# A decoder's expert stage: fp32 products replaced by three products of rounded halves, with the weights split ahead of time

## Chip, cores and metric

One NeuronCore of a Trainium2 chip runs the whole program as one launch. The metric is the device time of that launch in microseconds (us). TensorE is called PE (its weight loads PEld), VectorE DVE, ScalarE ACT, GpSimd POOL, and SyncE SP, which here issues most transfers.

## What is computed

The reference is a two-layer decoder on x of 4 x 512 tokens by 512 features: self-attention, cross-attention and a mixture of experts, then a second self-attention, cross-attention and a ternary feed-forward net. The change touches the mixture of experts and the first self-attention, in which its weights are prepared. The expert part, cut:

```python
h = x @ down_w + down_b                    # 512 -> 256
probs = softmax(x @ router_w + router_b - COST_LAMBDA * cost)
topv, topi = top_k(probs, 2); gate = softmax(topv)
for k in range(2):                         # 8 experts, hidden sizes 256, 512, 768, 1024, twice
    acc = sum over e of gelu(gelu(h * mask_e) @ w1_e + b1_e) @ w2_e + b2_e
    out = out + acc * gate[..., k]
```

All of it is fp32.

## The kernel before

The program is a row of stages. The profile has them at about these times: self-attention 0 from 0 to 460 us, cross-attention 0 to 540, mixture of experts to 1135, self-attention 1 to 1975, cross-attention 1 to 2640, the ternary net to the end.

The mixture routes 4096 token rows (2048 tokens, two experts each). It sorts them by expert into tiles of 256 rows (at most 23 and one spare, 24 turns in all) and cuts each expert's hidden layer into pairs of 128 columns. An *item* is one tile against one pair: `ITEMS` is 79, always. `which` holds, for each item, its tile and its pair, found on the chip.

- **Weights.** `pack_experts` (L781), called by GpSimd in self-attention 0, copies each of the 20 pairs from the inputs to `moe_items` in DRAM, 60 transfers. `load_item` (L974) on SP loads one item's first weight (L979) and its second weight with the bias (L982) into one of `SLOTS` = 3 buffers. The first half waits for `hidden` of item i-3, the second for `output` of item i-3.
- **Rows.** `turn_rows` on PE (L1154) transposes a tile; DVE's `keep_turned` (L1476) copies it from PSUM to `turned`. ACT's `take_tile` (L1253) copies the item's tile to `x_now`.
- **Products.** In PE's queue, item i's turn of the loop is `hidden(i + 1)` (L1165), then `output(i)` (L1176). Between the two of one item ACT applies Gelu (L1264). Each has four fp32 products of 256 columns, which the profile shows as two instructions each.
- **Sums.** DVE adds each item's result to its tile's row of `acc` (L1510), which GpSimd cleared before the loop (L1580). SP stores one tile of `acc` to `moe_mixed` (L993) when all its items are in, 23 times. After the loop GpSimd gathers each token's two rows (L1601).
- **Beside it.** In the same loop GpSimd loads one eighth of a ternary weight (L1591, 512 KB, 24 in all), DVE turns it into ternary form every third item (L1491 to L1497), and GpSimd stores it (L1589, 256 KB).

SP's queue in the loop is written out by hand; every wait in it holds up what stands behind it:

```python
            for i in range(SLOTS, ITEMS):
                if i + AHEAD < TILES:
                    load_rows(i + AHEAD)
                load_item(i)
                if (stored + 1) * max(PAIRS) + SLOTS <= i:
                    store_tile(stored)
                    stored += 1
```

In self-attention 0 GpSimd has, in this order, the split of `wo` into halves (L472, L474), which ACT waits for before its 7th copy of turned probabilities (L363), the small power of the first layer norm (L96), which DVE waits for, and then `pack_experts`.

Of the kernel before, what the change touches and what calls it, by code (L numbers as in the profile page):

```python
# [133 lines left out]
def self_attention_0(nc, m, x, Wq, bq, Wk, bk, Wv, bv, Wo, bo, packed, a):  # L134
# [18 lines left out]
    NEXT_X = TILES + 6  # L153
    Q0, SC = NT, TILES + 2 * NT
    TA, TV, MM = TILES // 2, TILES // 2, 3 * KD + 2 * GROUPS + NT
    with ExitStack() as ctx:
# [34 lines left out]
        s.out_rows_in, s.out_high, s.out_low, s.out_stored = (sem(n) for n in ("out_rows_in", "out_high", "out_low", "out_stored"))  # L191
        w_q, w_k, w_v, w_out, x_tok_loaded = sem("w_q"), sem("w_k"), sem("w_v"), sem("w_out"), sem("x_tok_loaded")
# [4 lines left out]
        def _(sp):  # L197
# [8 lines left out]
            sp.dma_start(m.x_tok[:], x.rearrange("b (j p) d -> p (b j) d", p=P)).then_inc(x_tok_loaded, 16)  # L206
# [16 lines left out]
            with sp.Fori(0, B - 1) as b:  # L223
                sp.wait_ge(x_tok_loaded, 16)
                sp.wait_ge(s.mm.full, b * MM + 3 * KD + 1)
                sp.dma_start(x_rows[:], m.x_tok[:, bass.ds(b * NT + NT, NT), :]).then_inc(s.x_loaded, 16)
                load_out(b)
                store_out(b)
# [153 lines left out]
        def _(dve):  # L382
            with dve.Fori(0, B) as b:
# [57 lines left out]
                dve.wait_ge(x_tok_loaded, 16)  # L441
# [27 lines left out]
        def _(pool):  # L469
            pool.wait_ge(w_out, 32)  # L470
            pool.wait_ge(s.max_ready, 1)
            pool.tensor_copy(wo_high[:], wo[:]).then_inc(s.wo_high_made, 1)  # L472
            pool.wait_ge(s.wo_high_made, 1)
            pool.tensor_tensor(wo_low[:], wo[:], wo_high[:].bitcast(F32), ALU.subtract).then_inc(s.wo_split, 1)  # L474
            layernorm_rstd(pool, st, 0, m, s)
            pack_experts(pool, packed, a)
# [283 lines left out]
FIRST = KL * LATENT  # L760
# [3 lines left out]
class Packed:  # L764


    def __init__(self, nc, ctx):
# [6 lines left out]
        self.wo1 = nc.dram_tensor("split_out", (HEADS1, P, 2, D), F32, kind="Internal").ap()  # L774
        self.items_in, self.cleared = ctx.enter_context(nc.semaphore("moe_items_in")), ctx.enter_context(nc.semaphore("moe_cleared"))


ITEM_LOADS = 3 * sum(PAIRS) * 16


def pack_experts(pool, packed, a):  # L781

    for e in range(EXPERTS):
        for n in range(PAIRS[e]):
            to, at = packed.items[PAIR0[e] + n], slice(n * 2 * P, (n + 1) * 2 * P)
# [47 lines left out]
def mixture_of_experts(nc, m, w, packed, a):  # L833
# [27 lines left out]
    with ExitStack() as ctx:  # L861
# [101 lines left out]
        def _(sp):  # L963
# [38 lines left out]
            for i in range(1, SLOTS):  # L1002
                load_item(i)
# [1964 lines left out]
```

## Time and profile before

| | us |
|---|---|
| median of 3 runs | 2902.24 (2897.63 to 2905.83) |
| span of the profiled execution | 2871.8 |
| outside that span, by the median | 30.4 |
| item loop, first product to last | 773.5 to 1062.9 |

The profiled execution has no time of its own beside its span. The span runs from the first to the last instruction, so a change is added to the median as it is found in the span. An engine's busy time joins overlapping instructions of a group; products on PE overlap one another by most of their shown duration, so the step between them is read from runs of several.

### The profile page before, as it was taken

Reading aid. Unit: us, or ns where it says so; the run is one execution under the profiler, and the core shown is the slowest. Engines: PE = TensorE matmul, PEld = TensorE weight load, DVE = VectorE, ACT = ScalarE, POOL = GpSimd, SP = SyncE. Lnnn points to the kernel's source line nnn. Section 1 sums busy time; section 2 is a strip of 40 time slices with the busy share of each in tenths; the row PEclk is TensorE's granted clock in tenths of the full one; section 3 lists DMA queues with packets and bytes.
Section 4 is the critical chain, followed back from the end, with each engine's and each line's share of the span. In section 5 each row is a group of like instructions: output and inputs, shape, how many; then the busy total and the mean of one; then the engine's idle time right before and its main releaser. Section 6 shows DMA issues by size and latency. Waiting matters only on the chain. (4 is left out here: it accounts for less than half of the span.)

```text
span 2871.8 us, 40570 instructions
## 1 busy us (share of the span) xinstructions
PE 2673.5 (93%) x12750; PEld 1685.2 (59%) x12750; DVE 1806.2 (63%) x3475; ACT 1420.3 (49%) x2978; POOL 294.5 (10%) x399
## 2 busy tenths in 40 slices
PE   8999997979999987999999999997999999997898
PEld 4555554444588863677777777775545455443444
DVE  5666674654543326756755756754777777775676
ACT  4454463322133322554553653743577676664665
POOL 1230003001711114000000000001110101000000
PEclk9999998989999999999999999998899999999999
DMA  3395105541687754323223223211000000001000
GB/s 140 86 123 143 58 15 184 186 141 54 200 277 234 248 184 148 115 103 109 73 106 110 68 104 124 66 67 59 5 6 6 5 2 5 2 2 71 26 23 30
DMA packets 114169, 266.30 MB, mean 93 GB/s; under 512 B 14464, under 2 KB 37008, under 8 KB 113200
## 3 DMA queue, kind: packets, MB, share of 16 engines
q1 hardware_dynamic: 97152, 211.16, 22.2%
q0 software_dynamic: 16816, 52.64, 7.8%
q8 instruction: 104, 1.70, 0.2%
q14 instruction: 97, 0.79, 0.1%
HBM read 208.97 MB, written 58.48 MB: 93 GB/s over the span
## 5 line engine op out<-in xcount | busy, mean ns | idle before, releaser
L2506 DVE TENSOR_REDUCE x_neg_max<-bank 128x1 f32<-128x512 f32 x512 | 327.1, 684 | 99.7 <-PE bank L2351 99.2
L2458 ACT ACTIVATE x_weights<-bank 128x512 f32<-128x512 f32 x512 | 279.1, 599 | 127.8 <-PE bank L2362 122.9
L1885 ACT ACTIVATE a_probs<-bank,a_neg_max 128x128 f32<-128x128 f32 (+3 forms) x256 | 136.1, 532 | 206.0 <-DVE a_neg_max L1979 202.0
L1785 PE MATMUL bank<-a_x_high,a_weights 128*128 128x512 f32 x640 | 218.3, 404 | 8.2 <-DMA a_weights<-split_qkv 2.3
L109 PEld LDWEIGHTS bank<-all_ident,a_probs 128*128 128x128 f32 x1200 | 151.5, 140 | 85.0 <-issue 47.0
L109 PE MATMUL bank<-all_ident,a_probs 128*128 128x128 f32 x1200 | 193.3, 273 | 3.0 <-ACT a_probs_t L1877 2.2
L1877 ACT COPY a_probs_t<-bank 128x128 f32<-128x128 f32 (+3 forms) x256 | 107.6, 420 | 144.2 <-PE bank L109 143.8
L1820 PE MATMUL bank<-a_k_cols,a_q_cols 128*128 128x128 f32 (+3 forms) x512 | 176.7, 434 | 0.4 <-DVE a_q_cols L1928 0.2
L1849 PE MATMUL bank<-a_wo,a_att_high 128*128 128x512 f32 x512 | 162.1, 398 | 3.9 <-DVE a_q_cols L1928 2.9
L1510 DVE TENSOR_TENSOR moe_acc<-bank,moe_acc 128x512 f32 x79 | 54.6, 692 | 171.1 <-PE bank L1176 170.5
L1165 PE MATMUL bank<-moe_gh_cols,moe_item 128*128 128x256 f32 x632 | 151.8, 383 | 3.0 <-DMA moe_item<-moe_items 2.7
L1176 PE MATMUL bank<-moe_item,moe_wide 128*128 128x256 f32 x632 | 149.4, 379 | 0.0
L1832 PE MATMUL bank<-a_probs_t,a_v_rows 128*128 128x512 f32 (+3 forms) x512 | 148.6, 433 | 0.0
L1264 ACT ACTIVATE moe_wide<-bank,moe_item 128x256 f32<-128x256 f32 x158 | 66.3, 471 | 161.6 <-PE bank L1165 129.1
L1785 PEld LDWEIGHTS bank<-a_x_high,a_weights 128*128 128x128 f32 x640 | 121.3, 189 | 39.6 <-issue 6.2
L1891 ACT ACTIVATE a_probs<-a_probs,a_inv_sum 128x128 f32<-128x128 f32 (+3 forms) x256 | 142.0, 555 | 2.7 <-DVE a_inv_sum L1984 2.7
L2351 PE MATMUL bank<-x_k_cols,x_q_cols 64*128 64x512 f32 x512 | 136.6, 498 | 3.5 <-DVE x_neg_max L2506 3.4
L1979 DVE TENSOR_REDUCE a_neg_max<-bank 128x1 f32<-128x128 f32 (+3 forms) x256 | 125.7, 491 | 18.8
L2384 PE MATMUL bank<-x_weights,x_v_rows 128*17 128x512 f32 x1024 | 135.7, 603 | 0.0
L1165 PEld LDWEIGHTS bank<-moe_gh_cols,moe_item 128*128 128x128 f32 x632 | 118.1, 191 | 22.9 <-DMA moe_item<-moe_items 7.4
L2362 PE MATMUL bank<-x_q_cols,x_k_cols 64*128 64x512 f32 x512 | 128.1, 419 | 3.2 <-ACT x_weights L2458 2.8
L1176 PEld LDWEIGHTS bank<-moe_item,moe_wide 128*128 128x128 f32 x632 | 119.9, 190 | 16.8 <-issue 0.3
(413 smaller groups left out, 5437.0 us busy)
## 6 DMA issues: line engine op xcount, KB each, us to landing
a_weights<-split_qkv SPq DMA_DIRECT2D x80, 512.0 KB, 3.6
moe_item<-moe_items SPq DMA_DIRECT2D x79, 257.0 KB, 3.8
moe_item<-moe_items SPq DMA_DIRECT2D x79, 256.0 KB, 3.7
a_wo<-split_out SPq DMA_DIRECT2D x8, 2048.0 KB, 7.8
a_wo<-split_out SPq DMA_DIRECT2D x16, 1024.0 KB, 9.9
split_qkv<-x_qkv_parts SPq DMA_DIRECT2D x12, 1024.0 KB, 5.1
moe_items<-in_L_ffn_e_w POOLq DMA_DIRECT2D x40, 256.0 KB
split_out<-a_turned SPq DMA_DIRECT2D x8, 1024.0 KB, 4.0
```

The lines of the kernel that those rows point to most:

```text
L109: last = pe.transpose(bank[:, c * P:(c + 1) * P], rows[:, c * P:(c + 1) * P], ident)
L1165: last = pe.matmul(bank(("hidden", i))[:, c * TOKENS:(c + 1) * TOKENS], weight[:, k, c * P:(c + 1) * P], x_now[:, i % 2, k * TOKENS:(k + 1 ...
L1176: last = pe.matmul(bank(("item", i))[:, j * LATENT:(j + 1) * LATENT], hid[:, i % 2, c * TOKENS + j * P:c * TOKENS + (j + 1) * P], weight[: ...
L1785: last = pe.matmul(mm[g % 2], weight[:, k, :], x[:, k, :], start=n == 0, stop=n == 3 * KD - 1)
L1820: pe.matmul(sc[n % 4][:, 0:t], q_cols[:, h % 2, j * P:t], k_cols[:, h // GROUP, 0:t], start=True, stop=True).then_inc(s.sc.full, 1)
L1832: last = pe.matmul(mm[g % 2][:, c * P:], v_rows[:, c, kv * HD1:(kv + 1) * HD1], probs_t[:, n % 2, c, c * P:], start=c == 0, stop=c == NT - 1)
L1849: last = pe.matmul(mm[g % 2], att[:, at, j * P:(j + 1) * P], wo[:, at, part, :], start=h == first and att is att_high and part == 0, stop= ...
L1885: act.activation(probs[:, n % SLOTS, 0:t], sc[n % 4][:, 0:t], ACT.Exp, bias=neg_max[:, n:n + 1], accum_out=row_sum[:, n:n + 1]).then_inc(s ...
L1891: act.activation(probs[:, i % SLOTS, 0:t1], probs[:, i % SLOTS, 0:t1], ACT.Copy, scale=inv_sum[:, i:i + 1]).then_inc(s.probs_ready, 1)
L2351: pe.matmul(score_banks[slot % 3], q_cols[rows, u % 2, pair, j * P:(j + 1) * P], k_cols[rows, u % 2, pair, :], start=True, stop=True).then ...
L2458: act.activation(weights[:, chunk % 2, k, :], weight_banks[slot % 2], ACT.Exp).then_inc(s.weight.free, 1)
L2506: dve.tensor_reduce(neg_max[:, g % 2, j, h:h + 1], score_banks[slot % 3], AX.X, ALU.max, negate=True) \
```

## The change

Every expert weight w is kept as two halves, w_high (w rounded to the type `fp32r`) and w_low (w - w_high), and so are the item's input and its hidden values. A product becomes high x high + high x low + low x high, as products of type fp32r, which the kernel's other stages use already (L1785, L1849).

1. **Split, once.** `pack_experts` goes. In self-attention 0 GpSimd loads a pair (two transfers), casts 128x1024 to the high half, subtracts 128x1024 for the low half, stores 1 MB to `moe_items`, copies the bias by a fourth transfer, 20 times. The split of `wo` comes after the sixth pair, the first layer norm's power after the thirteenth. The staging buffers lie in `m.x_tok` of batches 1 to 3, so SP loads those parts of x only after the last pair is stored, ahead of `load_rows(1)`.
2. **Items.** `FIRST` doubles: an item's two loads are 512 and 513 KB. `hidden` and `output` have 12 products each in place of 4. PE now runs `hidden(i + 2)` ahead of `output(i)`; SLOTS stays 3.
3. **Halves of the activations.** ACT's `take_tile` writes x_high, GpSimd subtracts for x_low (128x512). DVE copies Gelu's result to hid_high and subtracts for hid_low (`split_hidden`).
4. **Sums.** DVE adds item i to a running sum in one of 4 slots (`add_result`); the running sum starts anew with each tile. SP stores every item's sum (256 KB, 79 stores). GpSimd's clearing of `acc` goes; small DVE work and one small PE product find the new places.
5. **Moves.** `keep_turned` from DVE to ACT, 5 tiles ahead. The bias of x (L1583, 4 x 128x2048 on GpSimd) to the routing phase. SP's first item loads wait for the last `core` product.

```diff
-FIRST = KL * LATENT
+FIRST = 2 * KL * LATENT
...
-        self.mixed = nc.dram_tensor("moe_mixed", (SPARE * TOKENS, LATENT), F32, kind="Internal").ap()
+        self.mixed = nc.dram_tensor("moe_mixed", (ITEMS * TOKENS, LATENT), F32, kind="Internal").ap()
...
+            def split_pair(i):
+                (e, n), stage = pairs[i], stages[i % STAGES]
+                pool.wait_ge(s.pair_in[i % STAGES], (i // STAGES + 1) * 32)
+                pool.tensor_copy(stage[:, :, 0].bitcast(F32R), stage[:, :, 1]).then_inc(s.pair_high, 1)
+                pool.wait_ge(s.pair_high, i + 1)
+                pool.tensor_tensor(stage[:, :, 1].bitcast(F32R), stage[:, :, 1], stage[:, :, 0], ALU.subtract).then_inc(s.pair_low, 1)
+                pool.wait_ge(s.pair_low, i + 1)
+                pool.dma_start(packed.items[i][:, 0:2 * FIRST], stage.rearrange("p w l n -> p (w l n)")).then_inc(s.pair_stored[i % STAGES], 16)
...
+            for i in range(len(pairs)):
+                if i == OUT_SPLIT_AT:
...
+                if i == FIRST_NORM_AT:
+                    layernorm_rstd(pool, st, 0, m, s)
+                split_pair(i)
+                if i + 2 < len(pairs):
+                    if i >= 1:
+                        pool.wait_ge(s.pair_stored[(i - 1) % STAGES], ((i - 1) // STAGES + 1) * 16)
+                    load_pair(i + 2)
...
             for i in range(SLOTS, ITEMS):
                 if i + AHEAD < TILES:
                     load_rows(i + AHEAD)
                 load_item(i)
-                if (stored + 1) * max(PAIRS) + SLOTS <= i:
-                    store_tile(stored)
-                    stored += 1
+                if i >= ACC_SLOTS:
+                    store_result(i - ACC_SLOTS)
...
                     for k in range(KL):
-                        last = pe.matmul(bank(("hidden", i))[:, c * TOKENS:(c + 1) * TOKENS], weight[:, k, c * P:(c + 1) * P],
-                                         x_now[:, i % 2, k * TOKENS:(k + 1) * TOKENS], start=k == 0, stop=k == KL - 1)
+                        for w, x in ((w_high, high), (w_high, low), (w_low, high)):
+                            last = pe.matmul(bank(("hidden", i))[:, c * TOKENS:(c + 1) * TOKENS], w[:, k, c * P:(c + 1) * P],
+                                             x[:, k, :], start=n == 0, stop=n == 3 * KL - 1)
+                            n += 1
...
             hidden(0)
+            hidden(1)
             for i in range(ITEMS):
...
-                if i + 1 < ITEMS:
-                    hidden(i + 1)
+                if i + 2 < ITEMS:
+                    hidden(i + 2)
                 output(i)
...
+            def split_hidden(i):
+                dve.wait_ge(*emptied(("hidden", i)))
+                if i >= 2:
+                    dve.wait_ge(*filled(("item", i - 2)))
+                dve.tensor_copy(hid_high[:, i % 2, :], hid[:, i % 2, :])
+                dve.drain()
+                dve.tensor_tensor(hid_low[:, i % 2, :], hid[:, i % 2, :], hid_high[:, i % 2, :].bitcast(F32), ALU.subtract).then_inc(s.hid_ready, 1)
+
+            def add_result(i):
+                to = acc[:, i % ACC_SLOTS, :]
+                if i >= ACC_SLOTS:
+                    dve.wait_ge(s.stored[i % ACC_SLOTS], i // ACC_SLOTS * 16)
+                dve.wait_ge(*filled(("item", i)))
+                dve.drain()
+                if i == 0:
+                    dve.tensor_copy(to, bank(("item", i))).then_inc(free(("item", i)), 1)
+                else:
+                    dve.scalar_tensor_tensor(to, acc[:, (i - 1) % ACC_SLOTS, :], same[:, i:i + 1], bank(("item", i)), ALU.mult, ALU.add) \
+                       .then_inc(free(("item", i)), 1)
...
+            for i in range(ITEMS):
+                pool.wait_ge(s.x_high_ready, i + 1)
+                tile = pool.value_load(which[i:i + 1, 0:1], min_val=0, max_val=SPARE)
+                pool.tensor_tensor(x_low[:, i % X_SLOTS, :], turned[:, bass.ds(tile, 1), :].rearrange("p o n -> p (o n)"),
+                                   x_high[:, i % X_SLOTS, :].bitcast(F32), ALU.subtract).then_inc(s.x_now_ready, 1)
+                q, late = divmod(i - QUANT_FROM - STORE_LAG, QUANT_EVERY)
+                if late == 0 and 0 <= q < EIGHTHS_ALL:
+                    store_ternary(q)
```

## Rows read from the trace of the kernel before

**Rows 1.** The page, section 1: engine busy time, share of span, instructions.

```profile
PE 2673.5 (93%) x12750; PEld 1685.2 (59%) x12750; DVE 1806.2 (63%) x3475; ACT 1420.3 (49%) x2978; POOL 294.5 (10%) x399
```

**Rows 2.** Timeline in the item loop: start, duration, engine, line, count.

```profile
954.49 1.89 PE L1165 MATMUL bank<-moe_gh_cols,moe_item 128*128 128x256 f32 x8
...
956.22 1.89 PE L1176 MATMUL bank<-moe_item,moe_wide 128*128 128x256 f32 x8
...
957.94 1.89 PE L1165 MATMUL bank<-moe_gh_cols,moe_item 128*128 128x256 f32 x8
958.28 0.33 SPq L982 DMA_DIRECT2D moe_item<-moe_items  x1
...
958.65 0.43 SPq L993 DMA_DIRECT2D moe_mixed<-moe_acc  x1
...
959.84 0.33 SPq L979 DMA_DIRECT2D moe_item<-moe_items  x1
```

**Rows 3.** Windows: us, busy time by engine, PE clock, transfer share, GB/s.

```profile
773.00:870.00 97.00, 96.78 (x482) 84.25 (x481) 44.32 (x70) 37.13 (x78) 21.21 (x19) 0.99 0.82 258
...
1136.00:1157.00 21.00, 17.23 (x74) 13.29 (x73) 12.18 (x18) 0.00 (x0) 0.00 (x0) 1.00 1.02 410
```

**Rows 4.** Transfers from 773 to 1062 us: 40 slices, sum, issues with landing.

```profile
DMA  5598988898777786877787877886887886776562
GB/s 158 168 340 257 315 294 260 298 272 281 254 226 236 237 272 210 273 228 214 237 257 215 275 245 215 258 240 206 267 262 233 243 272 175 268 253 215 172 201 73
DMA packets 37735, 69.19 MB, mean 239 GB/s; under 512 B 3824, under 2 KB 13643, under 8 KB 37707
...
moe_item<-moe_items SPq DMA_DIRECT2D x76, 257.0 KB, 3.8
...
ternary<-ew_down POOLq DMA_DIRECT2D x24, 256.0 KB, 2.7
...
ew_core<-in_L_ffn_w_gate POOLq DMA_DIRECT2D x8, 512.0 KB, 6.7
```

**Rows 5.** Transfers of the whole span: the projection weights of self-attention 1.

```profile
a_weights<-split_qkv SPq DMA_DIRECT2D x80, 512.0 KB, 3.6
```

**Rows 6.** Timeline: products of type fp32r, 512 columns wide.

```profile
1703.17 0.62 PE L1785 MATMUL bank<-a_x_high,a_weights 128*128 128x512 f32 x2
1703.63 0.39 PE L1785 MATMUL bank<-a_x_low,a_weights 128*128 128x512 f32 x1
```

**Rows 7.** Timeline: four transposes of type fp32r, 128 columns wide, seen by their loads.

```profile
1999.00 0.40 PEld L109 LDWEIGHTS bank<-x_ident_r,x_split 128*128 128x128 f32 x4 [1.15 <-DVE x_swapped L2544]
```

**Rows 8.** Groups on GpSimd: busy us, mean ns, idle before.

```profile
L2589 POOL TENSOR_TENSOR x_split<-x_rot,x_split 128x512 fp32r<-128x512 f32 x32 | 41.0, 1280 | 423.4 <-ACT x_split L2442 423.4
...
L787 POOL DMA_DIRECT2D moe_items<-in_L_ffn_e_w x20 | 14.1, 703 | 0.0
...
L474 POOL TENSOR_TENSOR a_wo_low<-a_turned,a_wo_high 128x2048 fp32r<-128x2048 f32 x1 | 4.6, 4614 | 0.1
...
L472 POOL CAST a_wo_high<-a_turned 128x2048 fp32r<-128x2048 f32 x1 | 1.9, 1890 | 55.2 <-DVE a_neg_max L411 55.2
```

**Rows 9.** Timeline of GpSimd in self-attention 0: the first layer norm's power.

```profile
126.04 1.03 POOL L96 TENSOR_TENSOR a_ln_rstd<-a_ln_var_eps,all_minus_half 128x4 f32<-128x4 f32 x1 [62.62 <-DVE a_ln_var_eps L86]
```

**Rows 10.** Timeline of ACT in self-attention 0: its seventh copy of turned probabilities.

```profile
71.99 0.59 ACT L366 COPY a_turned<-bank 128x512 f32<-128x512 f32 x1 [1.07 <-PE bank L109]
```

**Rows 11.** Timeline, GpSimd beside DVE at the loop's start.

```profile
765.81 18.01 POOL L1583 TENSOR_TENSOR all_x_tok<-all_x_tok,ew_up_b 128x2048 f32<-128x2048 f32 x4
...
781.81 2.04 DVE L1483 TENSOR_SCALAR all_scale<-moe_abs_total 128x3 f32<-128x3 f32 x1
...
783.92 0.18 DVE L1485 RECIPROCAL moe_inv_scale<-all_scale 128x3 f32<-128x3 f32 x1
```

**Rows 12.** Groups on DVE: busy us, mean ns, idle before.

```profile
L391 DVE TENSOR_TENSOR a_k_low<-a_whole,a_high 64x512 fp32r<-64x512 f32 x64 | 43.9, 686 | 12.4 <-ACT a_high L340 11.7
...
L1491 DVE TENSOR_SCALAR ew_core<-ew_core,moe_inv_scale 128x1024 f32<-128x1024 f32 x24 | 17.8, 744 | 0.0
```

More of the change, by code:

```diff
@@ L469, in _ @@
         def _(pool):
[L470 to L476, printed above, removed]
+            stages = [m.x_tok[:, NT * (1 + i):NT * (2 + i), :].rearrange("p j d -> p (j d)").rearrange("p (w l n) -> p w l n", w=2, l=2)
+                      for i in range(STAGES)]
@@ new lines, in _, with load_pair @@
+            pairs = [(e, n) for e in range(EXPERTS) for n in range(PAIRS[e])]
+            def load_pair(i):
+                (e, n), raw = pairs[i], stages[i % STAGES][:, :, 1]
+                at = slice(n * 2 * P, (n + 1) * 2 * P)
+                pool.dma_start(raw[:, 0].rearrange("p (k n) -> p k n", k=KL), chunked(a[f"L0_ffn_e{e}_w1"][:, at])).then_inc(s.pair_in[i % STAGES], 16)
+                pool.dma_start(raw[:, 1].rearrange("p (c n) -> p c n", c=2), chunked(a[f"L0_ffn_e{e}_w2"][at, :])).then_inc(s.pair_in[i % STAGES], 16)
@@ L774, in __init__ @@
         self.wo1 = nc.dram_tensor("split_out", (HEADS1, P, 2, D), F32, kind="Internal").ap()
+        self.pair_in = [ctx.enter_context(nc.semaphore(f"moe_pair_in_{i}")) for i in range(PAIR_STAGES)]
+        self.pair_stored = [ctx.enter_context(nc.semaphore(f"moe_pair_stored_{i}")) for i in range(PAIR_STAGES)]
         self.items_in, self.cleared = ctx.enter_context(nc.semaphore("moe_items_in")), ctx.enter_context(nc.semaphore("moe_cleared"))
[L778 to L785, printed above, removed]
-            half = KL * LATENT
-            pool.dma_start(to[:, 0:half].rearrange("p (k n) -> p k n", k=KL), chunked(a[f"L0_ffn_e{e}_w1"][:, at])) \
-                .then_inc(packed.items_in, 16)
-            pool.dma_start(to[:, half:2 * half].rearrange("p (c n) -> p c n", c=2), chunked(a[f"L0_ffn_e{e}_w2"][at, :])) \
-                .then_inc(packed.items_in, 16)
-            pool.dma_start(to[:, 2 * half:PACKED], columns(a[f"L0_ffn_e{e}_b1"][at]), allow_slow_non_contiguous=True) \
-                .then_inc(packed.items_in, 16)
+ITEM_LOADS, PAIR_STAGES = sum(PAIRS) * 16, 3
 def moe_weights(nc, ctx):
@@ L1124, in _ @@
             last.then_inc(full("gates"), 1)
+            pe.wait_ge(s.same_ready, 1)
+            pe.wait_ge(*room("same"))
+            pe.matmul(bank("same")[:, 0:P], ones[:], below[:], start=True, stop=True).then_inc(full("same"), 1)
             pe.wait_ge(s.gb1_ready, EXPERTS)
@@ L1158, in hidden @@
             def hidden(i):
-                weight = item[:, i % SLOTS, 0:KL * LATENT].rearrange("p (k n) -> p k n", k=KL)
+                weight = item[:, i % SLOTS, 0:FIRST].rearrange("p (l k n) -> p l k n", l=2, k=KL)
+                w_high, w_low = weight[:, 0], weight[:, 1]
+                high, low = (x.rearrange("p (k t) -> p k t", k=KL) for x in (x_high[:, i % X_SLOTS, :], x_low[:, i % X_SLOTS, :]))
                 pe.wait_ge(s.first_in[i % SLOTS], (i // SLOTS + 1) * 16)
@@ L1353, in _ @@
             dve.tensor_tensor(over, others, own, ALU.is_gt)
-            dve.tensor_tensor(same, others, own, ALU.is_equal)
+            dve.tensor_tensor(equal, others, own, ALU.is_equal)
             dve.drain()
-            dve.tensor_tensor(same, same, before[:].unsqueeze(1).to_broadcast(shape), ALU.mult)
+            dve.tensor_tensor(equal, equal, before[:].unsqueeze(1).to_broadcast(shape), ALU.mult)
             dve.drain()
-            dve.tensor_tensor(over, over, same, ALU.add)
+            dve.tensor_tensor(over, over, equal, ALU.add)
             dve.drain()
@@ L1462, in _ @@
                 add_magnitudes(SUMS_EARLY + t - EARLY, 1)
+            dve.wait_ge(*filled("same"))
+            dve.tensor_copy(same[:], bank("same")[:, 0:ITEMS]).then_inc(free("same"), 1)
             dve.wait_ge(*filled("const"))
```

231 lines of the change are left out of this document (149 added, 82 removed).

## The prediction, made before the changed kernel was run

> **What bounds the kernel now.** I read the page first: PE is busy for 93% of the span [rows 1], so any work taken from PE should show unless something else fills its place. Then I went to the stage that the change touches, by its timeline, since the mean over 2872 us says nothing about it. In the item loop the reader should look at the starts of PE's groups of eight: 954.49, 956.22, 957.94 [rows 2]. They are 1.73 us apart with no gap, 0.216 us for each instruction, so an item costs PE 16 x 0.216 = 3.46 us. 79 items make 273 us, and with the 20 tiles that are transposed inside the loop (8 x 0.11 us each) the 289 us from 773.5 to 1062.9 are explained. The loop is bound by PE and by nothing else.
>
> Next the transfers of the same stretch. They are not idle: 82% busy at 258 GB/s while PE is 100% busy [rows 3], and 69.19 MB move in the loop, 239 GB/s on average [rows 4]. An item's load takes 3.8 us from issue to landing [rows 4], longer than an item, and costs nothing only because SP issues it two items before PE needs it. This is the number I take the forecast from: a loop that is bound by PE, but with transfers near four fifths of what they can do.
>
> **The change on PE.** 24 products of type fp32r replace 16 fp32 instructions. The trace has none that is 256 columns wide. At 512 columns two of them start within 0.46 us, 0.23 each [rows 6]; at 128 columns four take 0.40 us with the whole first load counted, so 0.10 at most [rows 7]. A straight line between the two gives 0.14 us at 256 columns. From below, one of the two passes that an fp32 instruction of 256 columns makes takes 0.216 / 2 = 0.108 [rows 2]. I take 0.13: 24 x 0.13 = 3.1 us an item, between 2.6 and 3.4. By PE alone the loop would fall by 79 x 0.35 = 27 us (5 to 68).
>
> **The change in the transfers.** Per item, in KB of 1024 bytes: two loads of 512 and 513 in place of 256 and 257; one store of 256 in place of 23 in 79 items; the ternary work stays at (512 + 256) / 3 = 256. That is 1537 KB, 1.57 MB, where the loop moved about 0.88 MB an item. In all: 79 x 1025 + 79 x 256 + 24 x 768 + 24 x 256 = 125,775 KB. Three items, seven tiles of rows and two raw eighths (5891 KB) are in before the first product. 119,884 KB, 122.8 MB, are left. At PE's pace of 3.1 us an item this asks for 508 GB/s, at the old 3.46 still for 455.
>
> What can the transfers do? The same 4 KB runs, loads alone on SP's queue, reach 410 GB/s with the share at 1.02 [rows 3]. That is the most in this trace. In the item loop, where loads, stores and GpSimd's queue mix, the three slices with a 9 among the first nine moved 340, 315 and 272 GB/s [rows 4]. So a full queue of this mix is worth 0.30 to 0.37 MB/us, and I take 0.33, near the rows of the same mix and not near the pure one: 122.8 / 0.33 = 372 us for the loop (332 at 0.37, 409 at 0.30, 300 at 0.41).
>
> The Trainium skill (DMA: Bandwidth & Descriptors, Specifications) puts the HBM limit of one core at about 358 GB/s. By it the loop would be 122.8 / 0.358 = 343 us, an estimate. The 410 GB/s of the trace are above that limit, so it doesn't hold for one busy core here; my number doesn't use it.
>
> **The same from the order of SP's queue.** PE's order becomes hidden(i), output(i-2), hidden(i+1), output(i-1). SP issues, once output(i-3) has ended: the second half of item i, the store of item i-4, then the first half of item i+1. Let L be the time from output(i-3)'s end to the landing of that first half; hidden(i+1) needs it after only hidden(i) and output(i-2), one item's work, where before it was two. So two items take L plus one item's PE work: T = (L + 3.1) / 2. L: the second half's issue to the first half's issue is 1.56 us today with a store between [rows 2], some 0.15 for the semaphore, 3.6 for 512 KB on a quiet queue [rows 5], and what is in front of it: 512 + 256 KB at 410 GB/s are 1.9 us, of which 1.5 have passed, plus GpSimd's 256 KB an item, 0.6. Together 6.3, T = 4.7 us, 79 T = 371 us. Both ways meet at 372, 83 us more than 289 (43 to 120). The third buffer is used up here: it is SLOTS that would have to grow.
>
> **What hides in the loop.** With T = 4.7, DVE has per item a copy of 512 elements (0.37 by half of L1491's 1024, 0.69 at most), two operations of 0.69, and the ternary third, about 0.6: 2.4 us. GpSimd has 1.28 [rows 8] and 0.4 of issues; ACT two Gelus, a copy, 1.5. All fit. Their chain to the next product has more than one item of slack: at T = 3.1 the split after a ternary step would end 0.4 us before PE asks for it. Off the path, cost nothing; if DVE became late it would be by 0.3 to 0.7 us an item.
>
> **Self-attention 0.** A pair costs GpSimd a cast of 1024 (0.95, half of L472), a subtraction (2.3, half of L474) and four issues of 0.7: 6.1 us, 6.8 with waits [rows 8]. It waits for w_v, then for its own loads; I put the first pair's landing at about 23 us. Six pairs end at 64, the split of wo 6.5 later at 70.5. ACT needs it at 71.99 [rows 10]: no slack, and 0.5 us more a pair is 3 us of wait. Seven more pairs end at 118; the layer norm's power is wanted at 126.04 [rows 9], so 8 us of slack, but GpSimd's queue is strict: at 9 us a pair it comes at 152, and DVE, then PE's next projections, wait 26 us. The last seven pairs end near 175; x for batches 1 to 3 then loads before batch 1, of some 115 us, ends.
>
> There is a second cost. GpSimd's work and DVE's get in each other's way: while GpSimd adds over 128x2048, 18.01 us for four, DVE's scaling of 128x3 takes 2.04 us, where its neighbour in line takes 0.18 [rows 11]. The Trainium skill (SBUF — State Buffer, Who interferes with whom) says why: the two share one pair of ports, held by one for a whole instruction, against DVE instructions with two inputs in SBUF or in a two-port mode. The trace agrees. Which work is exposed: the subtractions L391, 0.69 each [rows 12], four to a projection of 3.43 us, so DVE is as full as PE there. With GpSimd holding 3.3 of 6.8 us, about 14 us of k projections in each of two batches stretch by a quarter: 7 us (0 to 14). With 3 us of waits for wo I take +10 (0 to 40). The 60 transfers that `pack_experts` made ran beside PE's work and nobody waited for them in this stage, so their going gives nothing.
>
> **Start of the loop.** ACT copies five tiles in place of DVE's four, and the first x_low adds 1.3 us on GpSimd: +3 (0 to 6). The first items (3 MB) load once the last core product has ended, 9 us of transfer at 0.33, while PE and DVE still work on the gates and the constant rows. The x bias and the clearing were hidden by PE in their old place and are in the new one. The end of the loop is the same chain: last sum, store, gather.
>
> **Sum.** 83 + 10 + 3 = 96 us in the span of 2871.8, so a span near 2968; the median is 30.4 above the span, 2902.2 + 96 = 2998.
>
> **Rivals.**
> - *A. Forecast: transfers and the lead of one item set the pace*, T 4.2 to 5.2. Chance 0.62. 2998.
> - *B. Transfers keep nearly their best rate*, 0.36 to 0.41 MB/us. For it: pure loads do 410 and two thirds of the bytes are of that kind. Against: the 3 us behind every issue stay, and a full mixed slice has not passed 340. Loop 300 to 341, with +13: 2926 to 2967, say 2948. Chance 0.17. The page's 358 GB/s ends here too.
> - *C. PE cools, or GpSimd is late in self-attention 0.* With 1.6 us of wait for every 4.7, PE may be granted its lower clock of 1.2 GHz, where its products double: 24 x 0.24 = 5.8 us, T up to 6. For it: the loop has held 0.99 only at 100% busy [rows 3], and no row shows it with such pauses. Against: it would still be busy for two thirds, with each pause under 2 us. A third of the loop so costs some 30 us more; the late power 26. 3030 to 3080, say 3055. Chance 0.14.
> - *D. The other side: the transfers are hidden and PE sets the pace.* T = 3.1 to 3.4, the loop 262 to 285: -27 + 13, about 2888. It needs 1.57 MB in less than 3.46 us, over 455 GB/s; below 440 (122.8 MB in 279 us) it can't be faster at all. The trace's best is 410 in pure loads. Chance 0.04 for faster and 0.03 for a draw.
>
> **Numbers.** The likeliest is 2998. B to 2940 and C to 3060 take in the bounds of the rate (0.41 leaves 2926 outside, 0.30 gives 3035) and of self-attention 0; about 2 in 10 stay out. Within 0.3% (9 us), which is about what this kernel's measurement can tell from no change: 0.03. Faster 0.04, slower 0.93.
>
> **What would show it.** In the profile after: the item loop 350 to 400 us long; transfer share at or near 1 there with 300 to 350 GB/s; PE idle before `hidden`, released by the transfer of moe_item, 1 to 2 us an item; product starts 0.12 to 0.14 us apart; the first half's landing 4.5 us or more; DVE's L391 in some places at 1 to 3 us; GpSimd's power at 126 to 130. Wrong would be: no wait for moe_item (then D), a rate over 380 GB/s (B), a PE clock under 0.9 in the loop or a wait of ACT or DVE for GpSimd over 10 us before 160 us (C).

## The result: 8% slower, outside the range

The changed kernel took 3133.27 us (median of 4 runs, 3132.12 to 3135.69) against 2900.43 for the kernel before: ratio 1.0795, 95% interval 1.0779 to 1.0812. Forecast were 2998 us and a range of 2940 to 3060. The direction and the place were right, the size was not: +233 us instead of +96.

The profiled execution of before was no typical one. Its span was 2871.8 us and its own time must have been near that, since in every later execution the time is the span plus some 1.8 us; the timed ones took 2898 to 2906. The prediction read this as 30 us "above the span". The likeliest reason is a difference between chips: on two chips the kernel before took 2860 to 2881 us, on two others 2891 to 2917. So stages are compared here with a second profile of both kernels from chips of the quick kind (`b1_before`, span 2868.5; `a2_after`, 3109.7). Starts in us:

| | before, first profile | b1_before | after, first profile | a2_after |
|---|---|---|---|---|
| last layer-norm power of self-attention 0 | 462.3 | 469.6 | 492.8 | 493.3 |
| last power ahead of the expert stage | 593.1 | 598.9 | 622.9 | 622.7 |
| first hidden product of the item loop | 773.4 | 781.5 | 826.1 | 808.9 |
| last output product | 1062.4 | 1072.2 | 1324.3 | 1310.0 |
| span | 2871.8 | 2868.5 | 3130.7 | 3109.7 |

From the second and fourth columns: self-attention 0 +23.7, the stages up to the experts 0, up to the loop +3.6, the item loop +210.4 (501.1 against 290.7), after it +3.4; together 241.2. The two profiles of the kernel before differ in self-attention 0 as well, 462.3 against 469.6, for a reason that is open, so +23.7 is known to some 7 us only.

**The page and the windows after.** PE is busy for 87% of the span where [rows 1] had 93%, but for 2721 us where it was 2674, though the change was to give it less work.

```profile
PE 2721.1 (87%) x13384; PEld 1753.1 (56%) x13384; DVE 1938.2 (62%) x3629; ACT 1433.5 (46%) x3002; POOL 477.9 (15%) x514
```

Windows of the item loop (columns as in [rows 3]):

```profile
900.00:1000.00 100.00, 64.32 (x409) 61.17 (x408) 47.93 (x63) 27.22 (x58) 31.35 (x29) 0.81 0.84 269
...
1100.00:1200.00 100.00, 63.93 (x384) 61.96 (x384) 41.69 (x63) 22.25 (x48) 26.64 (x26) 0.76 0.75 253
```

PE is busy for 64 of 100 us where [rows 3] had 97 of 97, at a granted clock of 0.76 to 0.81 where it was 0.99. No engine is full, and neither are the transfers: their share is 0.75 to 0.84. Their sums over the loop, which answer to [rows 4]:

```profile
DMA packets 53180, 123.39 MB, mean 245 GB/s; under 512 B 4717, under 2 KB 29293, under 8 KB 53143
...
moe_item<-moe_items SPq DMA_DIRECT2D x76, 513.0 KB, 4.8
moe_item<-moe_items SPq DMA_DIRECT2D x76, 512.0 KB, 5.8
```

The bytes are as forecast (122.8 MB), but at 245 GB/s, not 330. When nothing is full, look for a circle of waits. Here it is, in the timeline (rows of SyncE's queue and of PE alone, cut):

```profile
1184.50 0.33 SPq L1023 DMA_DIRECT2D moe_item<-moe_items  x1
...
1184.88 0.43 SPq L1034 DMA_DIRECT2D moe_mixed<-moe_acc  x1
...
1186.07 0.34 SPq L1020 DMA_DIRECT2D moe_item<-moe_items  x1
...
1191.32 0.58 PE L1211 MATMUL bank<-moe_x_high,moe_item 128*128 128x256 f32 x1 [4.29 <-DMA moe_item<-moe_items]
1191.70 0.41 PE L1211 MATMUL bank<-moe_x_low,moe_item 128*128 128x256 f32 x1
1191.91 0.63 PE L1211 MATMUL bank<-moe_x_high,moe_item 128*128 128x256 f32 x2
...
1196.39 0.35 PE L1226 MATMUL bank<-moe_item,moe_hid_low 128*128 128x256 f32 x1
1196.58 0.28 PE L1211 MATMUL bank<-moe_x_high,moe_item 128*128 128x256 f32 x1
1196.70 0.28 PE L1211 MATMUL bank<-moe_x_low,moe_item 128*128 128x256 f32 x1
```

An output product ends at 1184.0. SyncE then issues the second half (L1023), the store (L1034) and only at 1186.07 the first half (L1020). PE has used up its one item of lead and waits until 1191.32. The 24 products that follow start some 0.214 us apart, those after 1196.58 0.12: PE works at the lower of its two clock levels (1.2 and 2.4 GHz) after the wait and at the upper one later. Two items take 7.3 us from the end of the output product to the end of the wait and 5.2 us for those 24 products: 12.5 us, 6.3 an item. The loop has 35 waits of PE of more than 3 us, about one for every two items.

**Self-attention 0 after.** GpSimd's pair (L496, L498) beside VectorE's halves of a key (L404); the first power, which answers to [rows 9]; and the group that answers to [rows 12]:

```profile
31.65 5.59 DVE L404 TENSOR_TENSOR a_k_low<-a_whole,a_high 64x512 fp32r<-64x512 f32 x4 [0.73 <-ACT a_high L353]
31.71 1.52 POOL L496 CAST all_x_tok<-all_x_tok 128x1024 fp32r<-128x1024 f32 x1
33.31 2.67 POOL L498 TENSOR_TENSOR all_x_tok<-all_x_tok 128x1024 fp32r<-128x1024 f32 x1
...
38.97 5.79 DVE L404 TENSOR_TENSOR a_k_low<-a_whole,a_high 64x512 fp32r<-64x512 f32 x4 [0.73 <-ACT a_high L353]
...
142.34 1.04 POOL L96 TENSOR_TENSOR a_ln_rstd<-a_ln_var_eps,all_minus_half 128x4 f32<-128x4 f32 x1 [13.30 <-DVE a_ln_var_eps L86]
```

```profile
L404 DVE TENSOR_TENSOR a_k_low<-a_whole,a_high 64x512 fp32r<-64x512 f32 x64 | 65.5, 1023 | 12.4 <-ACT a_high L353 11.7
```

Before, two of these groups stood so:

```profile
30.97 2.79 DVE L391 TENSOR_TENSOR a_k_low<-a_whole,a_high 64x512 fp32r<-64x512 f32 x4 [0.73 <-ACT a_high L340]
...
35.48 2.79 DVE L391 TENSOR_TENSOR a_k_low<-a_whole,a_high 64x512 fp32r<-64x512 f32 x4 [0.73 <-ACT a_high L340]
```

Four subtractions take 5.59 us where they took 2.79, and the groups come 7.3 us apart where it was 4.51. GpSimd waits 13.30 us for VectorE at 142.34, so it is not GpSimd that is late.

### The profile page after: what moved, and what is told of

It reads as the page before. It is cut to its first block and busy times, and to the rows that moved or that the text cites. A ratio compares the mean times of both kernels' runs of the same rounds, so it can differ in the third digit from the quotient of the medians.

```text
span 3130.7 us, 42359 instructions
## 1 busy us (share of the span) xinstructions
PE 2721.1 (87%) x13384; PEld 1753.1 (56%) x13384; DVE 1938.2 (62%) x3629; ACT 1433.5 (46%) x3002; POOL 477.9 (15%) x514
## 5 line engine op out<-in xcount | busy, mean ns | idle before, releaser
L2574 ACT ACTIVATE x_weights<-bank 128x512 f32<-128x512 f32 x512 | 279.1, 599 | 127.6 <-PE bank L2478 122.8
L1211 PE MATMUL bank<-moe_x_high,moe_item 128*128 128x256 f32 x632 | 177.3, 360 | 180.9 <-DMA moe_item<-moe_items 176.8
L1211 PEld LDWEIGHTS bank<-moe_x_high,moe_item 128*128 128x128 f32 x632 | 140.5, 258 | 191.2 <-DMA moe_item<-moe_items 186.7
L1582 DVE SCALAR_TENSOR_TENSOR moe_acc<-moe_acc,moe_same,bank 128x512 f32<-128x512 f32 x78 | 58.3, 748 | 239.3 <-PE bank L1226 237.4
L1323 ACT ACTIVATE moe_hid<-bank,moe_item 128x256 f32<-128x256 f32 x158 | 66.2, 470 | 289.3 <-DMA moe_item<-moe_items 157.9
L96 POOL TENSOR_TENSOR a_ln_rstd<-a_ln_var_eps,all_minus_half 128x4 f32<-128x4 f32 x8 | 8.2, 1019 | 1141.1 <-DVE a_ln_var_eps L2104 831.2
L1699 POOL TENSOR_TENSOR moe_x_low<-ew_w,moe_x_high 128x512 fp32r<-128x512 f32 x79 | 107.0, 1355 | 364.7 <-ACT moe_x_high L1310 274.9
L1226 PE MATMUL bank<-moe_item,moe_hid_high 128*128 128x256 f32 x632 | 141.9, 323 | 0.7 <-issue 0.7
```

The costliest lines, as they stand in the source:

```text
L1211: last = pe.matmul(bank(("hidden", i))[:, c * TOKENS:(c + 1) * TOKENS], w[:, k, c * P:(c + 1) * P], x[:, k, :], start=n == 0, stop=n == 3 ...
L1226: last = pe.matmul(bank(("item", i))[:, j * LATENT:(j + 1) * LATENT], x[:, i % 2, c * TOKENS + j * P:c * TOKENS + (j + 1) * P], w[:, c, :] ...
L2574: act.activation(weights[:, chunk % 2, k, :], weight_banks[slot % 2], ACT.Exp).then_inc(s.weight.free, 1)
```

## Experiments

All start from the changed kernel unless said otherwise. A ratio with an interval rests on four executions; where none is given, the time is that of a single one. Experiments 2, 5, 6 and `e3_no_subtract` leave out part of the data or of the work.

**1. The order of the halves (`e1_order`).** SyncE's loop becomes

```
load_half(i + 1, 0)   # first half, waits for hidden(i - 2)
load_half(i, 1)       # second half, waits for output(i - 3)
```

> The changed kernel with one thing moved: SyncE issues the first half of item i + 1 before the second half of item i, so it no longer queues behind a wait for the output of item i - 3. Same bytes, same products. Theory A (the item loop is a round trip of one transfer with a lead of about one item: 6.3 us an item is half of a landing of 5.8 us plus the products and waits around it): the lead grows to two items and the loop, 499 us now (826 to 1325), falls to what the bytes allow, 4.7 to 5.1 us an item, 370 to 405 us; the whole kernel 3005 to 3040 us. Theory B (123 MB at the 245 GB/s of this loop is already what the queues give for this mix of transfers): loop 490 to 505 us, kernel 3125 to 3140. Theory C (TensorE at 1.2 GHz sets the pace by itself, 24 products of 0.214 us): 5.1 us an item whatever the order, and the spacing of the products stays at 0.214 us.

2995.05 us, ratio to before 1.033 (1.0297 to 1.0363). The loop falls from 498 to 354.8 us, 4.49 an item: 143 us from a moved line, with the same bytes. Window of the loop:

```profile
1000.00:1060.00 60.00, 45.36 (x347) 41.75 (x345) 43.23 (x59) 19.95 (x44) 24.00 (x23) 1.00 1.02 376
```

Theory B is dead: the queues carry 376 GB/s. The granted clock is back at 1.00 without anything done for it, so theory C in its strict form is too. Theory A had 370 to 405 us and the kernel at 3005 to 3040: the loop gained more than it allowed, since the queues gave more.

**2. Nearly no bytes (`e2_few_bytes`).** After three items each transfer carries 16 of its columns, in the old order.

> The changed kernel, leaving out nearly all bytes of the item transfers after the first three items: each still issues its two transfers and waits for them, but they carry 16 of 2048 columns each (the products then work on the weights of the first three items). Theory A and B (transfers set the pace): the loop falls to TensorE's own pace, 24 products of 0.118 us and the transposes, 3.0 to 3.6 us an item, 240 to 285 us, and the kernel to 2880 to 2920 us. Theory C (TensorE at 1.2 GHz sets the pace, transfers do not): 5.1 us an item, 405 us, and 3040 us.

Loop 336.7 us, 4.26 an item, kernel 2974.20. A miss for all theories: with transfers of 8 KB the loop still is no faster than that. They need 2.0 us from issue to landing, and PE still waits for them 49 times, 67.5 us in all. But that circle alone would be 2.1 us to the issue, 2.0 to the landing and 24 products of 0.12, 6.9 us for two items, where 8.5 were measured. So something else takes part. VectorE is busy for 77 of 100 us in the window from 900 us, and its subtractions of the hidden halves take 0.69 us alone but 1.4 in the mean where they meet work of GpSimd; how much of the rest that explains was not separated.

**3. Issue at once (`e7_issue_at_once`).** The old waits, but the pair's number is read ahead of them and the store comes last, so that both halves are issued together (0.85 us for the two).

> The changed kernel with the old order of the two halves (the first half of item i + 1 still behind the wait for the output of item i - 3), but with nothing between the second half of item i and the first half of item i + 1: the pair's number is read ahead of the wait and the result is stored behind both. In the changed kernel SyncE lets 1.6 us pass there (1184.50 to 1186.07). Theory A (two items in the time of SyncE's 2 us, a landing of 5.2 us and one item's 24 products at 0.214 us, 12.4 us together): 1.6 us less in 12.4 to 12.6, 5.4 to 5.6 us an item, loop 425 to 445 us (499 now), kernel 3058 to 3080. Theory B (queues' throughput): loop unchanged, kernel 3125 to 3140.

3069.70 us, ratio 1.0675 (1.0636 to 1.0713); loop 464.8, 36 us below a2_after, where 55 to 75 were expected. The transfers now meet: the first halves landed in 6.5 us, the stores in 7.1 (5.8 and 5.3 in the changed kernel). That is 0.7 us more of landing against some 1.1 less between the two issues: more than half of what the issue gave was taken back.

**4. PE kept busy (`e13_kept_busy`).** In `hidden`, ahead of the wait for the first half:

```
for n in range(16 if i >= 2 else 0):
    pe.matmul(bank(("hidden", i))[:, 0:TOKENS], high[:, 0, 0:P], high[:, 1, :], start=True, stop=True)
```

> The changed kernel, and TensorE multiplies a resident tile 16 times into the hidden bank (overwritten by the real products) before it waits for each item's first half: 1.9 us at 2.4 GHz in a wait of 4.3 us that comes at every second item. Theory C' (the lower granted clock, 0.78 in the loop, and products 0.214 us apart come from the waits and lengthen the round trip by up to 2.3 us): the products after a wait are 0.12 us apart again in most items, the granted clock of 900 to 1200 us is over 0.90, and the loop is 480 to 505 us, as what the clock gives back is about what the extra products take in the items without a wait. Theory C'' (something else holds the clock down): spacing 0.214 us and clock 0.8 as now, loop 530 us or more.

PE does two thirds more products, and the kernel is faster: 3052.81 us against 3111.57 for the changed kernel on the same chip, loop 450.7 against 501.1. Timeline and window:

```profile
1000.58 2.06 PE L1207 MATMUL bank<-moe_x_high 128*128 128x256 f32 x16
1002.47 0.28 PE L1213 MATMUL bank<-moe_x_high,moe_item 128*128 128x256 f32 x1
1002.60 0.28 PE L1213 MATMUL bank<-moe_x_low,moe_item 128*128 128x256 f32 x1
...
1008.35 0.39 PE L1213 MATMUL bank<-moe_x_high,moe_item 128*128 128x256 f32 x1 [0.98 <-DMA moe_item<-moe_items]
```

```profile
1000.00:1100.00 100.00, 90.33 (x736) 87.81 (x735) 52.13 (x74) 25.14 (x56) 31.56 (x30) 1.00 0.87 285
```

The products after the wait are 0.12 us apart and the clock is 1.00. So the low clock was the waits' doing, and giving it back is worth 50 us of the loop after the extra products are paid for; expected was a draw. Only single executions stand behind this pair.

**5. What the engines need (`e5_order_few`).** Order of experiment 1, transfers of experiment 2.

> The changed kernel with SyncE's order as in the first experiment (first half of item i + 1 ahead of the second half of item i), and leaving out nearly all bytes of the item transfers after the first three items (16 columns each). Neither a round trip nor bytes hold it any more, so the loop shows what the engines need. Theory A: TensorE at 2.4 GHz, 24 products of 0.118 us and the transposes, 3.0 to 3.3 us an item, 240 to 265 us, kernel 2880 to 2905. Theory C (TensorE is held at 1.2 GHz by something else than its waits): 0.214 us a product, 5 us an item. Theory D (VectorE, whose subtraction of the hidden halves went from 693 to 1108 ns when only the bytes were taken away, is the next bound): 3.5 to 4.2 us an item, 280 to 330 us, TensorE waiting for the halves of the hidden tile.

Loop 284.0 us, 3.59 an item, kernel 2894.04 where the kernel before takes 2867 to 2881 on that chip: theory D at its lower edge. Window:

```profile
900.00:1000.00 100.00, 89.83 (x719) 86.34 (x718) 93.08 (x122) 39.06 (x86) 50.80 (x49) 1.00 0.55 164
```

VectorE is busy for 93%, more than PE with 90%. The waits of PE that are left carry no name in the profile, so that VectorE ends them is read from the shares. So even with its weights for nothing this loop is only 7 us shorter than the old one (290.7). The prediction's 27 us for PE alone were not to be had in this loop.

**6. A quarter of the item's bytes less (`e6_order_less`).** Order of experiment 1, without the low halves of the first matrix.

> The changed kernel with SyncE's order as in the first experiment, and leaving out the low halves of the first matrix from the item transfers after the first three items: 256 KB of 1025 KB an item less, 20 of 123 MB. Theory B' (with the longer lead the loop, 355 us at 350 to 393 GB/s, is bound by bytes): the loop falls in proportion, to 355 x 103/123 = 297 us, 290 to 310, kernel 2935 to 2955. Theory A' (it is still a round trip, only a longer one): the landing shortens by about 1 of 7 us, shared by more items, loop 335 to 350 us.

Loop 351.6 us (354.8 with all bytes): theory B' is refuted, and A', at 335 to 350, just missed. With three slots it is a round trip still.

**7. Another bias, another slot (`e8_bias_first`, `e9_four_slots`).** The one lets the gelu go ahead of the second half; the other sets `SLOTS = 4`.

> The changed kernel with the order of the first experiment, and each item's bias moved from the end of the second transfer to the start of the first, so that the gelu of an item no longer waits for its second half (the slot's first part is refilled only after that gelu). In the first experiment the loop took 355 us, and with 20 MB less 352, so not bytes but a longer round trip set it: three items in SyncE's issue, a landing of 6.4 us, gelu 1.0, split 1.5 and an output of 2 to 2.5. Theory A': the gelu and the split leave that chain, three items take 10.7 to 11.5 us, 3.6 to 3.8 us an item, unless the queues hold it first: 123 MB at the highest rate seen, 393 GB/s, are 315 us. Loop 305 to 330 us, 25 to 50 below the first experiment; the kernel about 3% to 2% above before, where the first experiment was 3.3%. Theory B' (bytes already set the first experiment's loop): 350 to 360 us.

> The changed kernel with the order of the first experiment and a fourth slot for items (in place of an unused reserve), so that every transfer is issued one item earlier. Theory A': four items in the 13.4 us of the round trip would be 3.4 us an item; VectorE's own need is 3.6 (284 us, when nearly no bytes were moved), and 123 MB at 393 GB/s are 4.0 us an item, 315 us: the loop lands at 305 to 330 us with the DMA share at 1.0 throughout, no matter that there is a slot more. Theory B': 350 to 360 us as before. If neither bytes nor VectorE hold it: 270 to 290.

The bias made it worse: ratio 1.0385 (1.0336 to 1.0435), loop 388.4 us. The slot's first part is now refilled only after the gelu, which makes that chain longer. What was gained on the second half did not show; which of the two chains sets experiment 1 stays open. The fourth slot: 2952.58 us, ratio 1.0178 (1.0132 to 1.0223), loop 320.1. Its window:

```profile
1000.00:1100.00 100.00, 81.74 (x614) 75.91 (x613) 75.95 (x103) 36.15 (x77) 44.87 (x44) 0.98 1.04 407
```

Now the transfers are full, at 379 to 407 GB/s, and a 512 KB half takes 8.6 us to land without anyone being held up as before. This is the bound that the prediction had expected at 330 GB/s and 372 us.

**8. Self-attention 0 (`e3_no_subtract`, `e4_late_pairs`).** The one leaves out `pool.tensor_tensor` of `split_pair` (L498); the other holds the pairs back until the first scores.

> The changed kernel, leaving out the 20 subtractions by which GpSimd makes the low halves of the expert weights in self-attention 0 (the stored low half is then the whole weight); casts, transfers and the order stay. Theory P (VectorE's subtractions of queries and keys, 64x512 from two SBUF operands, are held up while GpSimd works on SBUF: 1023 ns in the mean against 686 before): they fall back to 0.70 to 0.78 us each, the first scores start near 60 us, the first layer-norm power near 126 to 128 (142.3 now), the stage's last power near 465 (492.8 now), kernel 3103 to 3110 us. Theory Q (the transfers of the pairs, 20 MB in and 21 MB out, are what delays the stage): nothing moves by more than 3 us. Theory R (GpSimd is late for the work queued behind the pairs): the split of the output weights still ends at 76 us, and the first power stays at 138 or later.

> The changed kernel with GpSimd's first pair held back until the first scores are there; the output weights are split first, then seven pairs, the layer-norm power, and the other thirteen. Theory P (VectorE held up by GpSimd's work on SBUF): the queries and keys of batch 0 take VectorE 0.70 us a piece again, first scores near 60 us, first power at 127 to 132, batch 1's queries and keys are still held up, so of the 30 us the stage gets back 8 to 16; kernel 3117 to 3125 us. Against it works that the token rows of batch 1 wait for the last pair, which now ends near 215 us. Theory R (order on GpSimd): first power no earlier than 138, kernel 3130 or more.

Without the subtractions: first power 130.3, last 470.9 (142.3 and 492.8), kernel 3113.54, each a little later than theory P said (126 to 128, near 465, 3103 to 3110). Theory P, with the casts still in the way:

```profile
L404 DVE TENSOR_TENSOR a_k_low<-a_whole,a_high 64x512 fp32r<-64x512 f32 x64 | 51.0, 796 | 12.4 <-ACT a_high L353 11.7
```

Held back: the first power comes at 129.8, as P had it, but the second at 283.6 (271.4), since the token rows wait for the last pair. 3156.18 us, ratio 1.0881 (1.084 to 1.0921), slower than the changed kernel, where 3117 to 3125 were expected. P was right about the cause and I was wrong about the bill.

**9. Only beside the scores (`e10_windows`, `e11_all`, `e12_windows_rows`).** Four slots, and eight, seven and five pairs in the scores of batches 0, 1 and 2; e11 adds the bias of experiment 7; e12 issues the rows of batch 3 ahead of the wait for the last pair.

> The kernel with four slots, and in self-attention 0 GpSimd splits the expert weights only while scores are made, never while VectorE subtracts the halves of queries and keys: output weights first, eight pairs in batch 0, seven in batch 1, five in batch 2, the token rows of batches 1 to 3 loaded as their stages come free. Theory P (the stage's 21 to 30 us are VectorE held up by GpSimd's work on SBUF): the subtractions are back at 0.70 us, the last power of the stage comes at 468 to 478 instead of 490 to 493, and the kernel is 12 to 22 us faster than with four slots alone. Theory R (GpSimd's order and the late token rows cost as much as they save, as with the held-back pairs, where the second power came 12 us later): within 5 us of four slots alone.

> All of it: the order, the bias in the first transfer, four slots, and GpSimd's work in the scores' stretches. If bytes (393 GB/s) set the loop already with four slots alone, the bias adds nothing and it is within 5 us of the run without it; if the round trip of the second half still counts, up to 20 us faster. Against the kernel before: 25 to 50 us slower in every theory, as the loop cannot go below 315 us by bytes or 284 by VectorE, with 289 to 291 before, and self-attention 0 keeps some 8 us.

> The kernel with four slots and GpSimd's splitting only in the scores' stretches, as tried before, but SyncE issues the rows of batch 3 ahead of its wait for the last pair, which there held TensorE up for 24.7 us (a_x_rows at 356 us). Theory P (VectorE held up by GpSimd is the whole of the stage's loss): powers at 130, 250, 362 and 472 to 480 us (490 to 493 with the pairs as changed, 470 in the kernel before on one chip, 462 on another), kernel 12 to 20 us faster than with four slots alone, 1.2% to 1.4% above before. Theory R (pairs in any order cost it as much): last power at 488 or later.

Ratios 1.0251 (1.0202 to 1.0299), 1.022 (1.0172 to 1.0267), 1.0184 (1.0147 to 1.0221): none better than four slots alone. In e10 and e11 the last power came at 506.4 and 504.7, later than with the pairs as changed, and PE waited 24.7 us for the rows of a batch. In e12 VectorE is free:

```profile
L405 DVE TENSOR_TENSOR a_k_low<-a_whole,a_high 64x512 fp32r<-64x512 f32 x64 | 43.9, 686 | 12.4 <-ACT a_high L354 11.7
```

and the first two powers come at 131.3 and 253.1 (140.5 and 268.2 with four slots alone), but the third at 379.6 and the last at 490.3 (490.8). The waits of its batch 2 say why; both are for transfers that SyncE issues behind its wait for the last pair:

```profile
ACT a_turned L388 <- DMA a_high<-in_L_attn_Wo: 15.7, 1, 15.7
...
DVE all_x_tok L460 <- DMA all_x_tok<-in_x: 9.8, 1, 9.8
```

I had moved one of three. Theory P had the last power at 472 to 480; it came where theory R said, at 488 or later. That VectorE was held up is shown by its subtractions; that the stage gets its time back once all three transfers are free was not tried.

**10. The stretch before the loop (`b1_before`, `a2_after`).**

> The kernel before once more, to be profiled a second time: its profiled execution had a span of 2871.8 us, while the timed ones took 2892 to 2907, some 28 us more. Theory S (the waits of 12 to 20 us of VectorE before the item loop, while GpSimd scatters the rows, which the changed kernel and its variants show, belong to most executions of either kernel and were absent in the one profiled execution of before): this profile shows such a wait between the scatter's first and last transfer, its first hidden product comes at 793 to 803 instead of 773, and its span is 2890 to 2905; then some 22 us of the 259 by which the spans differ are not the change's. Theory T (the change makes them): no such wait, first hidden product at 773 within 4 us, and the missing time lies in another stage.

> The changed kernel once more, for a second profile. In its first profile VectorE waited 12.2 and 11.5 us while GpSimd scattered the rows, with TensorE's products long done; three experiments on one chip showed no such wait and a first hidden product 184 us after the last power, where it was 203. Theory S (the wait belongs to the chip, not to the change): it comes and goes with the chip, and the two kernels on one chip differ by 225 to 240 us whichever it is. Theory T (the change makes it): it is here again, 203 us.

In the first profile after, VectorE waited twice for nothing that shows, while GpSimd scattered the rows (first row below); in experiment 1, on the same kind of chip, 17.8 us; in a2_after not at all (second row).

```profile
L1379 DVE TENSOR_TENSOR all_x_tok<-bank,all_x_tok 128x512 f32<-128x512 f32 x16 | 10.8, 684 | 26.7 <-issue 12.2 <-remote 11.5 <-PE bank L1126 3.0
```

```profile
L1379 DVE TENSOR_TENSOR all_x_tok<-bank,all_x_tok 128x512 f32<-128x512 f32 x16 | 10.8, 687 | 13.3 <-PE bank L1126 13.3
```

Theory S: from the last power to the first hidden product the changed kernel and its variants take 203 to 208 us on the chips where the kernel before takes some 2900, and 184 to 188 where it takes 2870. Before was profiled only without the wait, so that it has it on the slower chips rests on its time, not on a trace. b1_before was expected at 2890 to 2905 by theory S and came out at 2868.5: it had run on a quick chip. Theory T had its first hidden product at 773 within 4 us; it came at 781.5.

## Why the prediction was wrong

**The bound before, and the rival that won.** That PE bound the old loop, that the transfers would take its place, that SyncE's order leaves one item of lead: right, and the last is the whole cause (experiment 1). Rival B, transfers near their best rate, came true only with a fourth slot (experiment 7), and rival D, PE setting the pace in a loop of 262 to 285 us, is reached at its upper edge only when nearly no bytes move, with VectorE the fuller engine and the kernel no faster (experiment 5).

**The step that failed** is "T = (L + 3.1) / 2", in both its terms, and the agreement of "both ways meet at 372". The form holds: 12.5 us for two items. L was put at 6.3 and measures 7.3: from the output's end to the first half's issue 2.1 us, not 1.7, and from there to the landing 5.2, not 4.6 (3.6 on a quiet queue and 1.0 of others' bytes). The products were put at 3.1 and measure 5.2, since PE's clock falls in the wait that the same formula forecasts. Together 9.4 against 12.5, 1.6 us an item, 79 x 1.6 = 123 us. That is nearly all of the miss in the loop (+210 against +83). Rival C named the falling clock, with 0.14 and "a third of the loop so costs some 30 us more"; against it stood "each pause under 2 us". The trace has about one pause of 4 us and more for every two items, and the granted clock is 0.76 to 0.81 in every 100 us of the loop. Two fifths of its products are 0.21 us apart; so rival C had the share of the loop about right, and the length of the pauses and their price too small. Of the 123 us, 83 are the products' part by this formula; what experiment 4 gave back is 50, with 16 more products in every item. Since the main case itself forecast that PE waits for a third of the time, the clock belonged into its formula and not beside it. The throughput estimate of 372 us then seemed to confirm the number; it was a bound of another kind that happened to be equal, and it too was off: full queues of this mix give 379 to 407 GB/s (experiment 7), not 330.

**PE's own term.** A product was taken as 0.13 us and takes 0.12 at the upper level: right. But "all fit" for the other engines was wrong. VectorE was put at 2.4 us an item and needs 3.3 (93 of 100 us at 3.59). In experiment 5 its cast of the hidden values takes 0.42 us where GpSimd computes nothing and 0.99 in the mean where they overlap, its subtraction 0.69 and 1.36, and the ternary steps are stretched too (L1598's 1.44 us at 1184.85 in the trace after).

**Self-attention 0.** Put at +10, range 0 to 40; it is +23.7. The mechanism was right and its size was not: VectorE held up by GpSimd was priced at 7 us and costs 21.6 in L404 alone (65.5 against 43.9 in [rows 12]). Two readings made it small. The projection of 3.43 us is that of the queries, with two subtractions; those of the keys came 4.51 us apart before, with VectorE idle for under 1 us in each, so VectorE set their pace and what it loses there is lost to the stage. And the stretch is not a quarter: in each key projection of batches 0 and 1 one or two of the four subtractions are held up, from 0.69 us to between 0.9 and 2.75. The wait for the split of the output weights did not come: the split ended at 76.3, 4.3 us after the time in [rows 10], but ACT's seventh copy was itself late by then (84.9), behind later scores, and waited for PE alone. The Trainium skill (SBUF — State Buffer, Who interferes with whom) says that one of the two holds the shared ports for a whole instruction. The trace agrees: the subtractions of 2.74 to 2.75 us in batch 0 all started during GpSimd's subtraction L498 and ended 0.54 to 0.55 us after it.

**The loop's start** was put at +3 and is +3.6.

**The sum.** The 30.4 us "above the span" are not a constant: in every later execution it is 1.8, and they most likely were a quicker chip. Taken to spans on like chips, +96 stands against +241.

## What to carry over

When no engine and no queue is full, find the circle: who issues the transfer, what that waits for, how long it lands, and what runs after it. A lead of one step is worth less than it looks, since landing times grow with load and PE came out of most waits of over 4 us at the lower of its clock levels. Two estimates that meet are no proof when both take durations from a kernel that did not wait.

Before a loop is given more bytes for fewer products, ask what it costs with the bytes for nothing. Here that was 284 us against 291, so no order of transfers could win more than 7 us. The best version tried, four slots with the first half issued ahead, is still 1.8% slower than the kernel before.

## What the runs showed of the hardware

- Useless products made a kernel faster: 16 more in every item, 50 us less in the loop.
- 512 KB took 3.6 us to land (median) in self-attention 1 [rows 5], 5.8 at 245 GB/s in the changed kernel, 7.2 at 350 in experiment 1 and 8.6 at about 400 with four slots.
- The transfers of the mixed loop reached 407 GB/s over 100 us. The Trainium skill (DMA: Bandwidth & Descriptors, Specifications) has about 358 GB/s as the HBM limit of one core; with one core running the program, the loop with four slots was above it, 378 GB/s on average.
- VectorE's subtraction of 64x512 takes 0.69 us alone and up to 2.75 when it starts during GpSimd's subtraction of 128x1024.
- The kernel before differs by 1% between chips (2860 to 2881, 2891 to 2917 us). In the trace after, 23.7 us of that kind are waits of VectorE during GpSimd's indirect transfers. What holds it there is open.
